# Cross attention: the second shifts between the products with values and those with ones, the second exponential ahead of the queries' eviction

## The chip, the cores and the metric

The kernel runs on one core of one Trainium2 chip. The metric is the device time in microseconds (us); lower is better. Engines are named as in the profile: PE is TensorE (PEld its weight loads), DVE is VectorE, ACT is ScalarE, POOL is GpSimd, SP is SyncE.

## The reference

A decoder of two layers on x of 32 batches x 128 rows x 128 channels. Layer 0 has self attention, cross attention to a context of 32 x 128 x 96, and gated experts; layer 1 has causal attention, a cross attention with latents, and routed experts. The change touches only the cross attention of layer 0:

```python
q = (query @ Wq + bq).reshape(B, Nq, H, D).transpose(0, 2, 1, 3)         # query: layernorm(x)
k = (key_value @ Wk + bk).reshape(B, Nkv, H, D).transpose(0, 2, 1, 3)    # key_value: ctx_768
v = (key_value @ Wv + bv).reshape(B, Nkv, H, D).transpose(0, 2, 1, 3)
attn = jnp.einsum('bhqd,bhkd->bhqk', q, k) * scale
attn = jnp.clip(attn, -CLAMP, CLAMP)
attn = jax.nn.softmax(attn, axis=-1)
x = jnp.einsum('bhqk,bhkd->bqhd', attn, v).reshape(B, Nq, Cq)
return x @ Wo + bo          # 16 heads of 8 channels; added to x
```

## The kernel before

One function, `attention`, does self and cross attention in one phase (and causal attention in a later one). The work goes by batch: numbers 0 to 31 are the batches of self attention, 32 to 63 those of cross attention. Four batches make a group, for which queries, keys and values are projected together.

Each engine runs its own list of steps, in order, and the lists are written out by hand in `ORDERS` (line 220 for cross attention). A step has a lead: in `AHEAD` (line 294), T and f0 at place n of the list work on batch n, s0 on batch n+2, w on batch n-1, y and a on batch n-2. A step written as `q^3` works on a whole group, three batches ahead of the group's first. So "round n" of all engines is T(n) and what stands around it. Semaphores between the engines do the rest: an engine that waits lets nothing behind the waiting step pass.

The steps that matter, with their lines:

- T, `key_scores` (TensorE, L437 to L442): twelve products, scores of batch n with keys on the partitions, into four banks of PSUM (`T` in the code). There is one set of these banks, so T(n) waits until both exponentials of batch n-1 have read them. It ends with four matmuls of L442.
- x0 and x1, `clip_scores` (VectorE, L636): clip to the bounds, in place, two banks each.
- s0, s1, `scores` (TensorE, L422): scores with queries on the partitions, two banks each time, for the maxima two batches ahead. m0, m1, `head_max` (VectorE, L630) reduce them; s1 waits for m0, as both use the same banks.
- mc (GpSimd, L811) clips the maxima; m on TensorE (L467) transposes them into the bank `OM`, and m on ScalarE (L564) copies them out, negated, as shifts.
- f0, f1, `shift` (TensorE, L454): two matmuls each that add the negated maxima of a query to all its scores, in two banks. f0 waits for x0, f1 for x1.
- e0, e1, `exps` (ScalarE, L557): the exponentials of two banks. e0 waits for f0, e1 for f1.
- w, `weigh` (TensorE, L488): 16 products of the exponentials of batch n-1 with the values, then 16 with ones (the sums of the softmax), both into halves of `OM`, and one semaphore at the end. w is free to start when e1 of n-1 is done and the maxima are copied out of `OM`.
- n, `normalise` (VectorE): waits for w; the reciprocal of the sums (L656) and the product with the heads (L660).
- y (TensorE, L501): the output projection of batch n-2; a (VectorE, L722) adds it to x.
- k, q, v on TensorE (L391 to L393): projections of a group, into one bank `PB` that y, the transposes and all projections share: each waits until the user before has been read out. k and q on ScalarE (L576) read keys and queries out of it, v on VectorE (L679) the values; kh and qh (L585) round them.
- mo (VectorE, L693 and L697): the moments of a later group's rows. km on GpSimd (L788) masks the keys by head.

The lists of a round were, with the leads applied: TensorE T s0 (k) m y (x) f0 w (q) f1 s1 (c) (v); ScalarE m (xh) (kh) e0 (q qh) e1 (ch) (ln) (k); VectorE (cs cl) x0 (mo) a x1 m0 (xl) n m1 (qs) (ks) (v). Steps in brackets come in one round of four; those of q, qh and mo in rounds 33, 37, 41 and so on (mo until 53, q until 57).

Of the kernel before, what the change touches and what calls it, by code (L numbers as in the profile page):

```python
# [18 lines left out]
ACT, ALU, AX = mybir.ActivationFunctionType, mybir.AluOpType, mybir.AxisListType  # L19

P = 128
B, D, DC = 32, 128, 96
H, DH = 16, 8
GB = 4
# [4 lines left out]
U = 4  # L29
# [84 lines left out]
def load_setup(nc, x, weights, cols, rows, consts, later, sb, sem, ready, routed):  # L114

    with ExitStack() as ctx:
# [102 lines left out]
    },  # L219
    "cross": {  # L220
# [4 lines left out]
    },  # L225
    "causal": {
# [14 lines left out]
def attention(nc, phase, kinds, sb, bank, context=None, x_ready=None):  # L241
# [27 lines left out]
    V, V_SUMS, maxes, head_ones = sb["v"], sb["v_sums"], sb["maxes"], sb["head_ones"]  # L269

    def one_pass(n):
        return kind(n) in ONE_PASS
# [9 lines left out]
    S, T = bank[:, 0:2 * GT], bank[:, 2 * GT:6 * GT]  # L282
    OM, PB = bank[:, 6 * GT:7 * GT], bank[:, 7 * GT:8 * GT]
# [5 lines left out]
    def t_bank(u):  # L289
# [1 line left out]

    AHEAD = {"T": 0, "f0": 0, "f1": 0, "y": -2, "s0": 2, "s1": 2, "m": 1, "w": -1, "e0": 0, "e1": 0, "x0": 0, "x1": 0,
             "m0": 2, "m1": 2, "n": -1, "a": -2, "mc": 1, "q0": 1, "q1": 1, "km2": 2, "km": 3}

    def steps(engine):


        for n in range(-10, NBT + 2):  # L300
            found = []
            for number, k in enumerate(kinds):
                order = ORDERS[k][engine].split()
                for place, step in enumerate(order):
                    name, _, lead = step.partition("^")
                    first = n + int(lead) if lead else n + AHEAD[name]
                    if first // B == number and not (lead and first % GB):
                        found.append((place / len(order), number, name, first // GB if lead else first))
            for _, _, name, i in sorted(found):
                yield name, i  # L310
# [15 lines left out]
    with ExitStack() as ctx:  # L326
        def buf(name, shape, dt=F32):
            return ctx.enter_context(nc.sbuf_tensor(f"{kinds[0]}_{name}", shape, dt))
# [20 lines left out]
        probs = [buf(f"probs{j}", [P, U, U, P]) for j in range(2)]  # L349
# [28 lines left out]
        def rows_of(u):  # L378
            return slice(32 * u, 32 * u + 32)
# [9 lines left out]
        def _(pe):  # L389
# [5 lines left out]
            def heads_free(n):  # L395

                if n > 0:
                    pe.wait_ge(heads_read if one_pass(n - 1) else heads_done, n)
# [13 lines left out]
            def scores(n, pair):  # L412
                causal = kind(n) == "causal"
                if pair == 0:
                    pe.wait_ge(k_masked, n + 1)
                if 2 * n + pair > 0:
                    pe.wait_ge(max_done, 2 * n + pair)
                units = (2 * pair, 2 * pair + 1)
                if causal:
                    hide([S[:, u * GT:(u + 1) * GT] for u in range(2)], P)  # L420
                for u in units:
                    mm = pe.matmul(s_bank(u), kq_hi[QUERY][(n // GB) % 2][rows_of(u), batch_cols(n)],  # L422
                                   k_hi_m[n % 2][rows_of(u), :, :], start=not causal, stop=True)
                mm.then_inc(scored, 1)

            def key_scores(n):
                causal, clip = kind(n) == "causal", kind(n) == "cross"
                pe.wait_ge(q_masked, 2 * n + 2)
                if n > 0:
                    pe.wait_ge(exp_done, 2 * n)  # L430
                g = (n // GB) % 2
                k_hi, k_lo, q_hi, q_lo = kq_hi[KEY][g], kq_lo[KEY][g], q_hi_m[n % 2], q_lo_m[n % 2]
                if causal:
                    hide([t_bank(u) for u in range(U)], 3 * P)
                out = [t_bank(u).rearrange("p (j q) -> p j q", j=U) for u in range(U)]
                for u in range(U):
                    pe.matmul(out[u], k_hi[rows_of(u), batch_cols(n)], q_hi[rows_of(u), :, :],  # L437
                              start=not causal, stop=False)
                for u in range(U):
                    pe.matmul(out[u], k_hi[rows_of(u), batch_cols(n)], q_lo[rows_of(u), :, :], start=False, stop=False)  # L440
                for u in range(U):
                    mm = pe.matmul(out[u], k_lo[rows_of(u), batch_cols(n)], q_hi[rows_of(u), :, :],  # L442
                                   start=False, stop=clip)
                    if clip and u % 2 == 1:
                        mm.then_inc(keyed, 1)

            def shift(n, pair):
                clip = kind(n) == "cross"
                if pair == 0:
                    pe.wait_ge(neg_max_done, n + 1)  # L450
                if clip:
                    pe.wait_ge(clipped, 2 * (n - B0) + pair + 1)
                for u in (2 * pair, 2 * pair + 1):
                    mm = pe.matmul(t_bank(u), cr[rows_of(u), C_ONES + u * P:C_ONES + (u + 1) * P],  # L454
                                   neg_max[n % 2][rows_of(u), :], start=False, stop=True, skip_group_check=clip)
                mm.then_inc(shifted, 1)

            def transpose_max(n):
                if kind(n) == "cross":
                    pe.wait_ge(max_clipped, n - B0 + 1)  # L460
                else:
                    pe.wait_ge(max_done, 2 * n + 2)
                if n > 0:
                    pe.wait_ge(neg_max_done, n)
                heads_free(n - 2)
                for j in range(U):
                    mm = pe.transpose(OM[:, j * P:(j + 1) * P], maxes[n % 2][:, j * P:(j + 1) * P], sb["ident"][:, :])  # L467
                mm.then_inc(max_transposed, 1)

            def weigh(n):  # L470
                pe.wait_ge(exp_done, 2 * n + 2)
                heads_free(n)
                pe.wait_ge(neg_max_done, min(n + 3, NBT))
                pe.wait_ge(pb_read, pb_uses["v", n // GB])
                if one_pass(n):
                    out = HEADS.rearrange("p (t a c) -> p t a c", a=2, c=32)
                    for j in range(U):
                        for u in range(U):
                            mm = pe.matmul(out[rows_of(u), :, j // 2, :], V_SUMS[(n // GB) % 2][:, n % GB, U * u + j, :],
                                           probs[n % 2][:, u, j, :].rearrange("p (t c) -> p t c", c=32),  # L480
                                           start=j % 2 == 0, stop=j % 2 == 1)
                    mm.then_inc(weighted, 1)
                    return
                for of, c in ((lambda u, j: V[(n // GB) % 2][:, n % GB, U * u + j, :], 0),
                              (lambda u, j: head_ones[:, j, :], P)):
                    for j in range(U):
                        for u in range(U):
                            mm = pe.matmul(OM[rows_of(u), c:c + P], of(u, j), probs[n % 2][:, u, j, :],  # L488
                                           start=j == 0, stop=j == U - 1)
                mm.then_inc(weighted, 1)  # L490

            def bank_free(name, i):
# [4 lines left out]
            def out_project(n):  # L497
                pe.wait_ge(heads_done, n + 1)
                bank_free("y", n)
                c = ATT[kind(n)] * P  # L500
                pe.matmul(PB[:, 0:P], o_t[n % 2][:, :], sb["w_out"][:, c:c + P], start=True, stop=True)\  # L501
                    .then_inc(out_projected, 1)
# [28 lines left out]
            for step, i in steps("PE"):  # L531
                if step == "T":
                    key_scores(i)
                elif step in ("f0", "f1"):
                    shift(i, int(step[1]))
                elif step == "y":
                    out_project(i)
                elif step in ("s0", "s1"):
                    scores(i, int(step[1]))
                elif step == "m":  # L540
                    transpose_max(i)
                elif step == "w":
                    weigh(i)
                elif step == "x":
                    transpose_x(i)
                elif step == "c":
                    transpose_c(i)
                else:
                    project(step, i)
# [2093 lines left out]
```

## Time and profile before

| | us |
|---|---|
| median of three runs | 1313.14 (1307.62 to 1318.99) |
| the profiled execution | 1306.53 |
| its span, first to last instruction | 1304.4 |
| mean granted clock of TensorE | 0.917 |

Shares of the span that each engine was busy: PE 83%, PEld 62%, DVE 73%, ACT 52%, POOL 61%. They are means over six stages with different limits; cross attention takes about a fifth of the span.

A row of a timeline gives the start and the length in us, the engine, the line, the operation, what it writes and reads, the number of instructions merged into the row, and in brackets how long the engine was idle before it and what ended that. An instruction may start a little before the end of the one before it on its engine, so the distance from start to start is the slot that it takes. Ends of matmuls are modelled.

### The profile page before, as it was taken

What the parts mean: (1) busy time and instruction counts of PE and PEld (TensorE: products, weight loads), DVE (VectorE), ACT (ScalarE), POOL (GpSimd) and SP (SyncE); (2) the same over time, 40 slices, a digit from 0 to 9 for tenths busy, and PEclk for the clock granted to TensorE, in tenths of its full rate; (3) what the DMA queues carried; (4) which work ended last, traced back from release to release, by engine and by line L of the source; (5) the groups of instructions that cost most, each with busy time, mean ns of one, the idle gap of its engine ahead of it and who ended that gap; (6) DMA issues with size and microseconds to landing.
All of it is one profiled execution on the core that took longest, in us unless ns stands there. A gap on an engine that the chain in (4) does not pass through costs nothing. (4 is left out here: it accounts for less than half of the span.)

```text
span 1304.4 us, 31319 instructions
## 1 busy us (share of the span) xinstructions
PE 1079.9 (83%) x11009; PEld 807.4 (62%) x11009; DVE 949.6 (73%) x2308; ACT 674.6 (52%) x1306; POOL 797.1 (61%) x895
## 2 busy tenths in 40 slices
PE   1799998888888887699978999994699888299992
PEld 0466665555555555566644666663598887299992
DVE  3598887479999996666644777775599976566764
ACT  2345554334455543345534655654789755166661
POOL 4788885535655651444436767762878687675662
PEclk9999999569999998699996999997799999599996
DMA  9930000000000000000000000000001001367765
GB/s 345 381 130 2 2 2 7 9 15 16 16 16 16 16 10 2 1 1 1 1 1 1 2 3 3 2 3 14 19 8 30 5 26 38 117 197 233 224 213 199
DMA packets 51705, 75.79 MB, mean 58 GB/s; under 512 B 13134, under 2 KB 31699, under 8 KB 51296
## 3 DMA queue, kind: packets, MB, share of 16 engines
q1 hardware_dynamic: 43488, 61.09, 14.7%
q0 software_dynamic: 4544, 8.47, 1.8%
q10 hardware_dynamic: 3520, 4.23, 0.9%
q8 instruction: 90, 1.47, 0.4%
q14 instruction: 63, 0.52, 0.1%
HBM read 40.89 MB, written 31.70 MB: 56 GB/s over the span
## 5 line engine op out<-in xcount | busy, mean ns | idle before, releaser
L630 DVE TENSOR_REDUCE maxes<-bank 128x8 f32<-128x1024 f32 x192 | 233.6, 1217 | 46.8 <-PE bank L422 45.5
L557 ACT ACTIVATE self_probs<-bank 128x1024 f32<-128x1024 f32 x128 | 129.1, 1022 | 45.7 <-PE bank L454 45.3
L788 POOL TENSOR_TENSOR self_k_hi_m<-self_kq_hi,const 128x512 fp32r<-128x512 f32 x64 | 66.5, 1038 | 73.4 <-ACT self_kq_hi L585 73.4
L1540 POOL DMA_INDIRECT returned<-relu_y,relu_slots x78 | 81.0, 1039 | 47.3 <-DVE relu_y L1512 32.8
L564 ACT ACTIVATE self_neg_max<-bank 128x512 fp32r<-128x512 f32 x64 | 38.2, 597 | 135.6 <-PE bank L467 135.6
L1458 ACT ACTIVATE relu_hidden<-bank,cols 128x256 f32<-128x256 f32 x156 | 74.1, 475 | 44.1 <-PE bank L1427 41.0
L1435 PE MATMUL bank<-relu_w_tiles,relu_hidden 128*128 128x128 f32 x624 | 95.0, 275 | 0.0
L1435 PEld LDWEIGHTS bank<-relu_w_tiles,relu_hidden 128*128 128x128 f32 x624 | 83.4, 192 | 0.0
L636 DVE TENSOR_SCALAR bank<-bank 128x1024 f32<-128x1024 f32 x64 | 78.2, 1224 | 3.3 <-PE bank L442 3.2
L2422 POOL DMA_INDIRECT routed<-latent_rows,latent_place_i x64 | 62.6, 978 | 24.4 <-issue 22.2
L454 PE MATMUL bank<-self_neg_max,const_r 32*128 32x512 f32 x256 | 63.7, 488 | 8.8 <-DVE bank L636 5.7
L1314 POOL TENSOR_TENSOR ffn_hidden<-ffn_product,ffn_gate 128x512 f32<-128x512 f32 x32 | 40.9, 1278 | 43.4 <-ACT ffn_gate L1072 35.5
L788 POOL TENSOR_TENSOR self_q_hi_m<-self_kq_hi,const 128x512 fp32r<-128x512 f32 x64 | 66.5, 1040 | 0.2 <-PE bank L454 0.2
L788 POOL TENSOR_TENSOR self_q_lo_m<-self_kq_lo,const 128x512 fp32r<-128x512 f32 x64 | 66.5, 1039 | 0.2 <-issue 0.2
L467 PE MATMUL bank<-ident,maxes 128*128 128x128 f32 x384 | 66.1, 297 | 0.5 <-POOL maxes L811 0.3
L557 ACT ACTIVATE causal_probs<-bank 128x1024 f32<-128x1024 f32 x64 | 63.7, 1022 | 3.6 <-PE bank L454 2.2
L467 PEld LDWEIGHTS bank<-ident,maxes 128*128 128x128 f32 x384 | 43.5, 147 | 33.1 <-issue 26.7
L422 PE MATMUL bank<-self_k_hi_m,self_kq_hi 32*128 32x512 f32 x256 | 60.3, 460 | 4.0 <-DVE maxes L630 2.6
L437 PE MATMUL bank<-self_q_hi_m,self_kq_hi 32*128 32x512 f32 x256 | 33.9, 506 | 34.5 <-ACT self_probs L557 32.8
L788 POOL TENSOR_TENSOR causal_q_lo_m<-causal_kq_lo,const 128x512 fp32r<-128x512 f32 x32 | 33.5, 1047 | 44.8 <-PE bank L454 44.7
L1425 PE MATMUL bank<-relu_s_hi,relu_w_hi 128*128 128x256 f32 x156 | 57.2, 367 | 1.0 <-DVE relu_s_lo L1488 0.9
L2399 POOL TENSOR_TENSOR latent_inverse<-latent_norms_kept,latent_power 128x6 f32<-128x6 f32 x32 | 42.6, 1331 | 13.9 <-DVE latent_norms_kept L2073 13.9
(409 smaller groups left out, 3523.4 us busy)
## 6 DMA issues: line engine op xcount, KB each, us to landing
relu_w_tiles<-in_w_ffn SPq DMA_DIRECT2D x39, 512.0 KB, 3.9
routed<-blank SPq DMA_DIRECT2D x1, 19760.0 KB, 61.4
relu_slots<-routed SPq DMA_DIRECT2D x39, 130.0 KB, 3.1
x_all<-in_x SPq DMA_DIRECT2D x8, 256.0 KB, 8.3
x_before<-x_all SPq DMA_DIRECT2D x8, 256.0 KB
relu_w_tiles<-returned SPq DMA_DIRECT2D x4, 512.0 KB, 8.0
latent_mask_rows<-returned ACTq DMA_DIRECT2D x4, 512.0 KB, 8.5
self_ctx_in<-in_ctx SPq DMA_DIRECT2D x8, 192.0 KB, 2.4
```

The source lines that it names most:

```text
L422: mm = pe.matmul(s_bank(u), kq_hi[QUERY][(n // GB) % 2][rows_of(u), batch_cols(n)], k_hi_m[n % 2][rows_of(u), :, :], start=not causal, sto ...
L454: mm = pe.matmul(t_bank(u), cr[rows_of(u), C_ONES + u * P:C_ONES + (u + 1) * P], neg_max[n % 2][rows_of(u), :], start=False, stop=True, sk ...
L467: mm = pe.transpose(OM[:, j * P:(j + 1) * P], maxes[n % 2][:, j * P:(j + 1) * P], sb["ident"][:, :])
L557: act.activation(probs[n % 2][:, 2 * pair:2 * pair + 2, :, :].rearrange("p u j q -> p (u j q)"), T[:, 2 * pair * GT:(2 * pair + 2) * GT], ...
L630: dve.tensor_reduce(out.rearrange("p j u -> p u j"), S.rearrange("p (u j k) -> p u j k", u=2, j=U), AX.X, ALU.max, negate=True).then_inc(m ...
L636: dve.tensor_scalar(t, t, CLAMP / scale, -CLAMP / scale, ALU.min, ALU.max).then_inc(clipped, 1)
L788: pool.tensor_tensor(out[n % 2][:, :, :], src[(n // GB) % 2][:, batch_cols(n)].bitcast(F32).unsqueeze(1).broadcast_to([P, U, P]), slots.un ...
L1425: pe.matmul(out, w_hi[t % 2][:, of], s_hi[t % 2][:, :], start=True, stop=False)
L1435: mm = pe.matmul(YT[t % 2][b][:, 0:P], hidden[i % C1][:, b * P:(b + 1) * P], w_tile[t % NW][:, F1 + c * P:F1 + (c + 1) * P], start=c == 0, ...
L1458: act.activation(hidden[i % C1][:, :], HT[i % 2][:, 0:TT], ACT.Relu, bias=sb["cols"][:, bass.ds(r + (COL_RELU + c), 1)]).then_inc(hidden_d ...
L1540: pool.indirect_dma_start(returned[:, :], bass.IndirectOffsetOnAxis(ap=slots[t % NX][:, b, P:P + 1].bitcast(I32), axis=0), y[t % NY][:, b, ...
L2422: pool.indirect_dma_start(routed[:, :], bass.IndirectOffsetOnAxis(ap=place_i[u % 3][:, k, b:b + 1], axis=0), rows[G % 4][:, k, n % GB, :], ...
```

## The change

On TensorE, w is cut in two steps: wv, the 16 products with values, with the waits of w, and ws, the 16 products with ones, with the semaphore. f1 stands between them. The projection of the queries, q, stands behind ws, and so behind f1, instead of ahead of f1. On ScalarE, e1 stands ahead of q and qh instead of behind them. On VectorE, the moments mo stand behind a and x1 instead of between x0 and a. No instruction is added or taken away, and no wait. Self and causal attention keep their lists; the cut applies to batches 32 to 62 as weighed in rounds 33 to 63.

```diff
--- before.py
+++ after.py
@@ -218,9 +218,9 @@
         "POOL": "qt^3 bo^6 rs^8 kl^2 km2 kt^4 q1 ql^2 q0",
     },
     "cross": {
-        "PE": "T s0 k^3 m y x^4 f0 w q^3 f1 s1 c^4 v^3",
-        "ACT": "m xh^4 kh^3 e0 q^3 qh^3 e1 ch^4 ln^5 k^4",
-        "DVE": "cs^3 cl^3 x0 mo^7 a x1 m0 xl^4 n m1 qs^1 ks^2 v^3",
+        "PE": "T s0 k^3 m y x^4 f0 wv f1 ws q^3 s1 c^4 v^3",
+        "ACT": "m xh^4 kh^3 e0 e1 q^3 qh^3 ch^4 ln^5 k^4",
+        "DVE": "cs^3 cl^3 x0 a x1 mo^7 m0 xl^4 n m1 qs^1 ks^2 v^3",
         "POOL": "kl^1 ql^1 mc q1 q0 km bo^2 rs^5",
     },
     "causal": {
@@ -291,7 +291,7 @@
 
 
 
-    AHEAD = {"T": 0, "f0": 0, "f1": 0, "y": -2, "s0": 2, "s1": 2, "m": 1, "w": -1, "e0": 0, "e1": 0, "x0": 0, "x1": 0,
+    AHEAD = {"T": 0, "f0": 0, "f1": 0, "y": -2, "s0": 2, "s1": 2, "m": 1, "w": -1, "wv": -1, "ws": -1, "e0": 0, "e1": 0, "x0": 0, "x1": 0,
              "m0": 2, "m1": 2, "n": -1, "a": -2, "mc": 1, "q0": 1, "q1": 1, "km2": 2, "km": 3}
 
     def steps(engine):
@@ -481,12 +481,16 @@
                                            start=j % 2 == 0, stop=j % 2 == 1)
                     mm.then_inc(weighted, 1)
                     return
-                for of, c in ((lambda u, j: V[(n // GB) % 2][:, n % GB, U * u + j, :], 0),
-                              (lambda u, j: head_ones[:, j, :], P)):
-                    for j in range(U):
-                        for u in range(U):
-                            mm = pe.matmul(OM[rows_of(u), c:c + P], of(u, j), probs[n % 2][:, u, j, :],
-                                           start=j == 0, stop=j == U - 1)
+                for j in range(U):
+                    for u in range(U):
+                        pe.matmul(OM[rows_of(u), 0:P], V[(n // GB) % 2][:, n % GB, U * u + j, :], probs[n % 2][:, u, j, :],
+                                  start=j == 0, stop=j == U - 1)
+
+            def weigh_ones(n):
+                for j in range(U):
+                    for u in range(U):
+                        mm = pe.matmul(OM[rows_of(u), P:2 * P], head_ones[:, j, :], probs[n % 2][:, u, j, :],
+                                       start=j == 0, stop=j == U - 1)
                 mm.then_inc(weighted, 1)
 
             def bank_free(name, i):
@@ -539,8 +543,10 @@
                     scores(i, int(step[1]))
                 elif step == "m":
                     transpose_max(i)
-                elif step == "w":
+                elif step in ("w", "wv"):
                     weigh(i)
+                elif step == "ws":
+                    weigh_ones(i)
                 elif step == "x":
                     transpose_x(i)
                 elif step == "c":
```

## Rows read from the trace of the kernel before

**Rows 1.** windows of the steady part: start:end, length, then busy us of PE, PEld, DVE, ACT, POOL

```profile
298.00:498.00 200.00, 165.75 (x2513) 115.56 (x2514) 188.10 (x280) 97.94 (x139) 113.89 (x143) 1.00 0.05 15
```

**Rows 2.** waits, steady part: who waited for whom, us in total, times, longest

```profile
DVE values L679 <- PE bank L393: 2.6, 6, 0.4
DVE self_recip L656 <- PE bank L488: 1.8, 6, 0.3
DVE bank L636 <- PE bank L442: 1.5, 6, 0.2
DVE x_all L722 <- PE bank L501: 1.2, 1, 1.2
PE bank L437 <- ACT self_probs L557: 18.1, 27, 1.0
```

**Rows 3.** timeline, VectorE, batch 43: x0, x1, m0, reciprocal, next x0

```profile
354.51 1.22 DVE L636 TENSOR_SCALAR bank<-bank 128x1024 f32<-128x1024 f32 x1
355.84 1.23 DVE L636 TENSOR_SCALAR bank<-bank 128x1024 f32<-128x1024 f32 x1
356.97 1.22 DVE L630 TENSOR_REDUCE maxes<-bank 128x8 f32<-128x1024 f32 x1
358.33 0.96 DVE L656 RECIPROCAL self_recip<-bank 128x128 f32<-128x128 f32 x1
361.26 1.22 DVE L636 TENSOR_SCALAR bank<-bank 128x1024 f32<-128x1024 f32 x1
```

**Rows 4.** timeline, TensorE, batch 43: f0, values, ones, f1, s1, next T

```profile
355.88 0.50 PE L454 MATMUL bank<-self_neg_max,const_r 32*128 32x512 f32 x2 [0.43 <-ACT self_neg_max L564]
356.31 1.08 PE L488 MATMUL bank<-self_probs,values 128*32 128x128 f32 x32
357.21 1.06 PE L488 MATMUL bank<-self_probs,head_ones 128*32 128x128 f32 x32
358.20 0.50 PE L454 MATMUL bank<-self_neg_max,const_r 32*128 32x512 f32 x2
358.53 0.40 PE L422 MATMUL bank<-self_k_hi_m,self_kq_hi 32*128 32x512 f32 x2
359.90 0.50 PE L437 MATMUL bank<-self_q_hi_m,self_kq_hi 32*128 32x512 f32 x4 [0.97 <-ACT self_probs L557]
```

**Rows 5.** timeline, VectorE, batch 45: moments, a, x1, values step, next x0

```profile
370.49 0.86 DVE L693 BATCH_NORM_STATS2 self_stats<-x_all 128x6 f32<-128x128 f32 x4
371.82 0.29 DVE L722 TENSOR_TENSOR x_all<-bank,x_all 128x128 f32<-128x128 f32 x1
372.03 1.22 DVE L636 TENSOR_SCALAR bank<-bank 128x1024 f32<-128x1024 f32 x1
377.35 0.89 DVE L679 TENSOR_TENSOR values<-bank,rows 128x128 f32<-128x128 f32 x4 [0.43 <-PE bank L393]
378.49 1.23 DVE L636 TENSOR_SCALAR bank<-bank 128x1024 f32<-128x1024 f32 x1 [0.25 <-PE bank L442]
```

**Rows 6.** timeline, TensorE, batch 45: q, v, next T

```profile
374.02 0.49 PE L391 MATMUL bank<-self_x_hi,w_hi 128*128 128x512 f32 x1
375.76 0.33 PE L391 MATMUL bank<-w_hi,self_c_hi 96*128 96x128 f32 x1
377.49 0.51 PE L437 MATMUL bank<-self_q_hi_m,self_kq_hi 32*128 32x512 f32 x4 [0.17 <-ACT self_probs L557]
```

**Rows 7.** timeline, VectorE, batch 57: a, without moments ahead of it

```profile
464.05 0.29 DVE L722 TENSOR_TENSOR x_all<-bank,x_all 128x128 f32<-128x128 f32 x1 [1.24 <-PE bank L501]
```

**Rows 8.** windows (columns as rows 1, then granted clock), and timeline of TensorE, batch 33

```profile
270.00:278.00 8.00, 6.28 (x45) 3.99 (x45) 4.49 (x14) 2.83 (x4) 2.08 (x3) 0.50 0.10 25
...
276.53 1.94 PE L488 MATMUL bank<-self_probs,values 128*32 128x128 f32 x32
278.24 1.93 PE L488 MATMUL bank<-self_probs,head_ones 128*32 128x128 f32 x32
```

**Rows 9.** timeline, VectorE, batch 63: x0

```profile
503.61 1.23 DVE L636 TENSOR_SCALAR bank<-bank 128x1024 f32<-128x1024 f32 x1 [1.30 <-PE bank L442]
```

## The prediction

> **What bounds the kernel now.** I read the busy time of each engine in the cross stage first, then the waits of VectorE and TensorE there, then the timeline of one batch on each engine. Batches are numbered as the program does: 0 to 31 are self attention, 32 to 63 cross attention. The change touches only cross attention, which runs from about 262 to 513 us of the span.
>
> In the steady part, 298 to 498 us, VectorE is busy 188.10 of 200 us, TensorE 165.75, ScalarE 97.94, at a granted clock of 1.00, the 2.4 GHz level [rows 1]. What the reader is to see is that 6% of idle time is all VectorE has to give. Its waits there that the profile names add up to 7.1 us, and the first clip of a batch (x0), the one that needs the new scores, waited for TensorE six times for 1.5 us in all [rows 2]. TensorE itself waited 18.1 us, 27 times, for the second exponential before it could start the next batch's scores [rows 2]. So there are two loops, and they are not equally tight. The scores step T needs e1 of the batch before, and that wait is visible on TensorE. But T's product is next read by VectorE's x0, and x0 stands in VectorE's queue behind m1 of the batch before, which is what sets its time. The wait on TensorE is idle time of an engine that doesn't set the pace.
>
> One plain batch (43) shows the order on VectorE: x0 at 354.51, x1 at 355.84, m0 at 356.97, the reciprocal of n at 358.33 [rows 3]. On TensorE: f0 at 355.88, the products with values at 356.31, those with ones at 357.21, f1 at 358.20, s1 at 358.53, and T at 359.90, after 0.97 us of waiting for e1 on ScalarE [rows 4]. Note the reciprocal: back to back, VectorE starts the next instruction 1.13 us after one of these (355.84 to 356.97), so n could have started at 358.10, and it starts at 358.33. It already waits 0.23 us for the products with ones, which end just before it. There is no slack ahead of n for those products to be later.
>
> **The split of the products (every batch from 33 on).** Nothing is added or removed in number: 16 products with values, 2 shifts, 16 products with ones. Only the order changes, and e1 and n change places as to who is served first. For batch 43:
> - The second shifts need x1, which ends at 357.07 (355.84 + 1.23); the same step after x0 came 0.15 us after the clip's end (354.51 + 1.22 = 355.73, f0 at 355.88), so f1 may start at about 357.22 [rows 3, 4].
> - They stand behind the products with values, whose slot before a shift I take as 0.99 us, as the ones' slot before f1 had it (357.21 to 358.20). So f1 starts at 356.31 + 0.99 = 357.30, which is 0.90 us earlier than before [rows 4].
> - The products with ones then start one slot of shifts later. From a shift to these products the slot is 0.43 us (355.88 to 356.31). That makes 357.73 instead of 357.21: 0.52 us later [rows 4].
> - The reciprocal was waiting for them already, so it starts 0.52 us later, and the sum's second part, the second maxima m1, and x0 of the next batch follow on VectorE at their old distances. The cost is 0.52 us on the path that sets the pace.
> - e1 and with it T can start earlier. This gives nothing back, because x0 stands behind m1, not behind T.
>
> The lower bound of that term takes the slots of pieces of equal shape: 0.90 from values to ones, and 0.33 from f1 to s1 [rows 4]. With these, f1 starts at 357.22, when x1's wait allows it, and the ones at 357.55: 0.34 us later. The upper bound gives the shifts their whole recorded 0.50 us and a gap of 0.10 more, 0.62 us. I take 0.52, since the slots from which it is made are for exactly these neighbours.
>
> The Trainium skill bears on this point, TensorEngine Tiling (Array Packing), Tiling Modes, Key Properties: a change of the tiling mode drains the array. Shifts use 32 rows by 128 columns and the products 128 rows by 32, so the new order changes mode twice more per batch. The slots here agree in size with about 0.1 us for each change (0.43 against 0.33, and 0.99 against 0.90); with that rule the term is 0.52, without it 0.34.
>
> **The moments, moved behind the second clip (five batches: 37, 41, ... 53).** In batch 45 they fill VectorE from 370.49 to 371.82, 1.33 us, between x0 and the addition of the output a, and x1 follows at 372.03 [rows 5]. It looks as if x1 could come 1.33 us earlier. It can't: a stands ahead of x1 and waits for the output projection, which waits for the eviction of the keys. Batch 57 has no moments, and there a waited 1.24 us [rows 7]. So the moments had been covering a stall; moved, the stall is bare and the moments push m0, n and m1 by 1.33 us. Two later waits, 0.43 us ahead of the values step v and 0.25 us ahead of x0, take up 0.68 of that [rows 5]: +0.65 us.
>
> **The queries' projection and eviction (batches 37 to 57, six with the full clock).** The same +0.65 us comes out on TensorE: f1 waits for x1's end (372.03 + 1.22 + 0.15 = 373.40), the ones start 0.43 later, the projection q 0.99 after that, at 374.82 instead of 374.02. The eviction is no longer behind a long queue on ScalarE, but the projection of v needs its bank free, so the 1.74 us from q to v (374.02 to 375.76) remain, and v is 0.80 us later; T saves its 0.17 us wait for e1, which leaves 0.63 [rows 5, 6]. The two paths run side by side, so they are not added: 0.65 us per such batch, batch 57 included by the second path. The mask of the next group's keys on GpSimd comes about as much later with the rounding of the queries; it is used a batch later. Bounds: 0.43 (one slot of shifts), and 1.33 if nothing is taken up.
>
> **The sum.** Batches 34 to 61 are 28: 22 plain x 0.52 = 11.4, and 6 x 0.65 = 3.9, together +15.3 us. Batch 33 runs at the lower clock, where TensorE is the slower engine and the order matters little; the last batches are bound by e1 after all (x0 of batch 63 waited 1.30 us for T [rows 9]), but the products with ones of that batch, and with them n, are late by the slot again. I take both at zero, between -1.3 and +0.5. The bounds are 22 x 0.34 + 6 x 0.43 - 1.3 = +8.8, and 22 x 0.62 + 6 x 1.33 = +22.
>
> The profiled execution took 1306.53 us (span 1304.4, so 2.1 lie around it): with the sum, 1321.8. The three runs shown have a median of 1313.14, that is 6.6 more, and go from 1307.62 to 1318.99. The mean of all four is 1311.6; I put the sum on that: **1327 us**, 1.2% slower.
>
> **Rivals.**
> - Faster: the loop T, clips, f1, e1, T sets the pace. For it: the 18.1 us that TensorE waits for e1 [rows 2]. e1 comes 0.90 us earlier, x 28 = 25 us less, 1287 us. It decides only where VectorE has run dry before x0; it did so in six of 26 batches, for 0.25 us each [rows 2]. Chance 0.06.
> - No measurable change: the slot of shifts costs its lower bound, or n's delay is taken up by waits that I have not seen. +4 to +9 us, about 1318 us. For it: the whole effect is a fraction of a microsecond per batch, and the sum stands close to the limit of 1%. Against it: VectorE has no idle time to take it up. Chance 0.34.
> - The forecast, +10 to +22 us, through VectorE's wait ahead of n. Chance 0.54.
> - Slower still: longer gaps on TensorE bring its clock to the 1.2 GHz level for part of the stage. At a granted clock of 0.50, the values' slot took 1.71 us (276.53 to 278.24) instead of 0.90 [rows 4, 8], so the two groups of products would end 1.6 us later; in a third of 28 batches that is 15 us more, 1342 us. TensorE is busy 83% of the steady part at the higher level [rows 1], and the same work in 7.27 instead of 6.75 us a batch would leave it at 77%. Chance 0.06.
>
> **How the numbers follow.** About 1% is what a measurement of this kernel can tell from no change. Slower by over 1%: 0.54 + 0.06 = 0.60; within 1%: 0.34; faster: 0.06. The range reaches from 1310 (almost the kernel before, so that most of the second rival is in) to 1340 (the upper bound of the sum and the spread of the runs); the forecast's own range is 1321 to 1334.
>
> **What would show it.** In the changed kernel VectorE's wait ahead of the reciprocal should appear in nearly every batch, some 0.7 us by the gap from the end of m0, or 15 us and more over the stage; its wait ahead of a should be about 1.2 us in batches 37, 41, ... 53; TensorE's wait for the second exponential ahead of T should be nearly gone; a plain batch should take 7.2 to 7.3 us from x0 to x0 instead of 6.75 (354.51 to 361.26, [rows 3]). If the reciprocal starts as early as before, the first term falls; if x0 comes earlier in spite of it, VectorE was not the bound; if a no longer waits, the second term falls.

## The result: 4.4% slower, nearly four times the forecast

The changed kernel takes 1371.61 us (four runs, 1370.55 to 1374.83) against 1312.86 us; the ratio is 1.0443, with a 95% interval of 1.0405 to 1.0481. The direction was forecast, the size was not: 1327 us and a range to 1340 us. The profiled execution took 1371.88 us, its span is 1369.8 us against 1304.4, and the mean granted clock of TensorE is 0.880 against 0.917. Here and below a ratio leaves out single runs that were over 1.5% above the fastest of the same kernel, a median does not. Lines behind the cut `weigh` stand six further down (clips L642, maxima L636, reciprocal L662, a L728), and the products are L486 (values) and L492 (ones).

First the part that came as forecast. VectorE in batch 42, a plain one, in the timeline of the changed kernel (columns as in [rows 3]):

```profile
372.32 1.23 DVE L642 TENSOR_SCALAR bank<-bank 128x1024 f32<-128x1024 f32 x1
373.66 1.22 DVE L642 TENSOR_SCALAR bank<-bank 128x1024 f32<-128x1024 f32 x1
374.79 1.22 DVE L636 TENSOR_REDUCE maxes<-bank 128x8 f32<-128x1024 f32 x1
376.72 0.96 DVE L662 RECIPROCAL self_recip<-bank 128x128 f32<-128x128 f32 x1 [0.71 <-PE bank L492]
379.64 1.22 DVE L642 TENSOR_SCALAR bank<-bank 128x1024 f32<-128x1024 f32 x1
```

The reciprocal starts 4.40 us after x0, where it was 3.82 [rows 3], and waits 0.71 us for the products with ones. The next x0 comes 7.32 us after this one instead of 6.75. TensorE in the same batch (to be laid beside [rows 4]):

```profile
373.70 0.50 PE L454 MATMUL bank<-self_neg_max,const_r 32*128 32x512 f32 x2 [0.38 <-DVE bank L642]
374.13 1.08 PE L486 MATMUL bank<-self_probs,values 128*32 128x128 f32 x32
375.14 0.50 PE L454 MATMUL bank<-self_neg_max,const_r 32*128 32x512 f32 x2
375.57 1.08 PE L492 MATMUL bank<-self_probs,head_ones 128*32 128x128 f32 x32
376.58 0.50 PE L422 MATMUL bank<-self_k_hi_m,self_kq_hi 32*128 32x512 f32 x2
376.85 0.51 PE L437 MATMUL bank<-self_q_hi_m,self_kq_hi 32*128 32x512 f32 x4
379.28 0.59 PE L422 MATMUL bank<-self_k_hi_m,self_kq_hi 32*128 32x512 f32 x2 [1.45 <-DVE maxes L636]
```

The slots are 1.01, 0.43 and 1.01 us. T starts 4.53 us after x0 instead of 5.39 and no longer waits for e1. But TensorE did not get faster by that: it now waits 1.45 us ahead of s0, for the maxima that VectorE makes later than before.

Then the part that was not forecast. Rounds of the changed kernel from x0 to x0, as windows (columns as [rows 8]): batches 36, 42, 43, 44, 45 and 49.

```profile
311.63:320.29 8.66, 6.87 (x100) 4.39 (x98) 7.76 (x11) 3.73 (x5) 3.82 (x5) 1.00 0.09 23
372.32:379.64 7.32, 5.49 (x92) 3.67 (x90) 6.57 (x8) 2.65 (x3) 6.50 (x8) 0.99 0.09 36
379.64:389.51 9.87, 8.35 (x92) 5.48 (x90) 6.67 (x9) 4.18 (x7) 4.88 (x9) 0.66 0.01 2
389.51:400.84 11.33, 9.65 (x100) 6.19 (x98) 7.87 (x12) 3.84 (x5) 3.83 (x5) 0.70 0.07 19
400.84:411.79 10.95, 10.04 (x108) 6.90 (x108) 8.26 (x20) 5.06 (x7) 3.03 (x5) 0.84 0.01 2
439.72:449.34 9.62, 8.69 (x108) 6.05 (x108) 8.08 (x21) 5.06 (x7) 3.05 (x5) 1.00 0.01 3
```

The four rounds of the kernel before that answer to batches 42 to 45, in the same view:

```profile
347.76:354.51 6.75, 5.38 (x92) 3.65 (x90) 6.57 (x8) 2.65 (x3) 6.28 (x8) 1.00 0.11 41
354.51:361.26 6.75, 5.32 (x92) 3.65 (x90) 6.57 (x10) 4.15 (x7) 4.87 (x9) 1.00 0.01 2
361.26:369.36 8.10, 6.60 (x100) 4.43 (x98) 7.76 (x12) 3.64 (x6) 3.82 (x5) 1.00 0.11 26
369.36:378.49 9.13, 8.29 (x108) 6.12 (x108) 8.13 (x21) 4.95 (x7) 3.28 (x5) 1.00 0.01 3
```

At a granted clock of 1.00 the rounds are 7.32, 8.66 and 9.62 us against 6.75, 8.10 and 9.13. But in 17 of the 28 rounds from 34 to 61 the clock is below 0.95 (in the kernel before in one, batch 35 at 0.78), and batch 43, with the same list of TensorE as 42, takes 9.87 us. There TensorE's slots are these:

```profile
381.28 0.79 PE L454 MATMUL bank<-self_neg_max,const_r 32*128 32x512 f32 x2
382.00 1.94 PE L486 MATMUL bank<-self_probs,values 128*32 128x128 f32 x32
383.87 0.79 PE L454 MATMUL bank<-self_neg_max,const_r 32*128 32x512 f32 x2
384.59 1.92 PE L492 MATMUL bank<-self_probs,head_ones 128*32 128x128 f32 x32
```

1.87 us from values to f1 and 0.72 from f1 to ones, at the 1.2 GHz level, instead of 1.01 and 0.43. Since the reciprocal has no slack ahead of it, each of these lands on VectorE.

The waits of the changed kernel, 294 to 566 us, name the same chain (columns as [rows 2]):

```profile
DVE self_recip L662 <- PE bank L492: 52.0, 27, 3.3
...
PE bank L422 <- DVE maxes L636: 21.6, 18, 1.5
...
DVE x_all L728 <- PE bank L505: 10.8, 11, 1.6
...
PE bank L467 <- POOL maxes L817: 1.8, 1, 1.8
...
PE bank L437 <- ACT self_probs L563: 0.2, 1, 0.2
```

VectorE's wait for the ones was 1.8 us in all, in the 200 us of [rows 2], and is 52.0 in these 272; TensorE's wait for e1 was 18.1 us and is 0.2.

**Where the 65.4 us of the two spans are.** Batches 34 to 61 took 211.9 us and take 264.1. With every round at its length at the full clock (14 x 7.32, 6 x 8.66, 6 x 9.62, and for 60 and 61 6.71 and 7.12 from the run after_filled_full below) they would take 226.0. So 14.1 us are the longer rounds and 38.1 us the rounds at the lower clock. Ahead of batch 32 the changed kernel is 10.7 us later; 6.1 of that is there before 90 us, where both run the same list, so it is no effect of the change. The other 4.6 come between 219 and 262 us. There the change does reach one round of self attention: in the rounds from one kind to the other the two lists are merged by each step's share of its list's length, and as TensorE's list for cross attention has one step more, the queries' projection of the first group of cross attention stands behind w of batch 28 in round 29 instead of ahead of it. The 4.6 can't be put down to that: in the same stretch the run of the second exponential below, without this exchange, took 3.1 us longer than the kernel before, and the changed kernel with more work on VectorE, which has it, took no longer. Behind batch 63 it loses 2.2 us, and the remaining rounds, 33 and 62, make 0.2.

### The profile page after: what moved, and what is told of

It is laid out like the page before. It is cut to its first block and busy times, and to the rows that moved or that the text cites. A ratio compares the mean times of both kernels' runs of the same rounds, so it can differ in the third digit from the quotient of the medians.

```text
span 1369.8 us, 31319 instructions
## 1 busy us (share of the span) xinstructions
PE 1139.8 (83%) x11009; PEld 839.4 (61%) x11009; DVE 949.1 (69%) x2308; ACT 676.7 (49%) x1306; POOL 798.5 (58%) x895
## 5 line engine op out<-in xcount | busy, mean ns | idle before, releaser
L636 DVE TENSOR_REDUCE maxes<-bank 128x8 f32<-128x1024 f32 x192 | 233.3, 1215 | 51.1 <-PE bank L422 50.4
L422 PE MATMUL bank<-self_k_hi_m,self_kq_hi 32*128 32x512 f32 x256 | 66.5, 511 | 25.4 <-DVE maxes L636 24.1
L454 PE MATMUL bank<-self_neg_max,const_r 32*128 32x512 f32 x256 | 73.5, 566 | 8.5 <-DVE bank L642 5.3
L642 DVE TENSOR_SCALAR bank<-bank 128x1024 f32<-128x1024 f32 x64 | 78.1, 1223 | 0.1
L662 DVE RECIPROCAL self_recip<-bank 128x128 f32<-128x128 f32 x32 | 30.6, 957 | 57.0 <-PE bank L492 57.0
L817 POOL TENSOR_SCALAR maxes<-maxes 128x16 f32<-128x16 f32 x32 | 7.0, 219 | 105.8 <-DVE maxes L636 105.8
L422 PEld LDWEIGHTS bank<-self_k_hi_m,self_kq_hi 32*128 32x128 f32 x256 | 27.7, 205 | 56.7 <-issue 44.8
```

What stands on the lines that cost most here:

```text
L636: dve.tensor_reduce(out.rearrange("p j u -> p u j"), S.rearrange("p (u j k) -> p u j k", u=2, j=U), AX.X, ALU.max, negate=True).then_inc(m ...
L642: dve.tensor_scalar(t, t, CLAMP / scale, -CLAMP / scale, ALU.min, ALU.max).then_inc(clipped, 1)
```

## The experiments

The theory after the result: the cut delays VectorE's reciprocal as forecast (about 15 us), and the rest is TensorE's clock. The rivals: that the waits alone make it, that another part of the change does, or that the clock is a companion and not a cause.

**The cut of the products alone.** Against the changed kernel, q stands ahead of f1 again (and so ahead of the ones too), and ScalarE's and VectorE's lists are those of before:

```diff
-        "PE": "T s0 k^3 m y x^4 f0 wv f1 ws q^3 s1 c^4 v^3",
-        "ACT": "m xh^4 kh^3 e0 e1 q^3 qh^3 ch^4 ln^5 k^4",
-        "DVE": "cs^3 cl^3 x0 a x1 mo^7 m0 xl^4 n m1 qs^1 ks^2 v^3",
+        "PE": "T s0 k^3 m y x^4 f0 wv q^3 f1 ws s1 c^4 v^3",
+        "ACT": "m xh^4 kh^3 e0 q^3 qh^3 e1 ch^4 ln^5 k^4",
+        "DVE": "cs^3 cl^3 x0 mo^7 a x1 m0 xl^4 n m1 qs^1 ks^2 v^3",
```

> The cut of the products alone: f1 between values and ones on TensorE in every round, the queries' projection still ahead of f1, ScalarE's and VectorE's lists as before. Theory (the split moves VectorE's reciprocal by about 0.55 us a batch, and the gaps that this makes on TensorE let its clock fall to 1.2 GHz in the stage): most of the loss, 1345 to 1375 us, mean granted clock of a cross round well under 1.00 in many rounds. Rival A (VectorE's wait alone, and the clock falls because of the moments' or the queries' move): +13 to +16 us, 1326 to 1329 us, clock 1.00 in nearly all cross rounds. Rival B (the split costs nothing by itself): 1313 us.

Measured: ratio 1.0343 (1.0285 to 1.0401), some 45 us, median 1357.82 us, granted clocks of 0.87 to 0.89 where the kernel before had 0.91 to 0.92. Most of the loss comes with the cut alone, as the theory said; rivals A and B fall.

**The moments alone.** The kernel before with VectorE's list of the changed kernel:

```diff
-        "DVE": "cs^3 cl^3 x0 mo^7 a x1 m0 xl^4 n m1 qs^1 ks^2 v^3",
+        "DVE": "cs^3 cl^3 x0 a x1 mo^7 m0 xl^4 n m1 qs^1 ks^2 v^3",
```

> The moments behind the second clip, all else as before. Theory: the addition of the output now waits some 1.2 us in five rounds, and a round with moments takes 0.65 us longer: +3 us, 1316 us, clock as before. Rival (the bare stall in these rounds is what lets the clock fall): +15 us or more and granted clocks under 1.00 in the rounds that follow.

Measured: ratio 1.0066 (1.0025 to 1.0106), 8.7 us, median 1322.70 us. That is between the two expectations. The profile (windows of batches 41 and 45, then VectorE's timeline in batch 37) shows why:

```profile
338.06:347.39 9.33, 8.48 (x108) 6.10 (x108) 7.90 (x20) 4.95 (x7) 2.84 (x5) 1.00 0.01 2
368.98:381.17 12.19, 11.76 (x108) 8.55 (x108) 8.27 (x21) 5.06 (x7) 3.67 (x6) 0.68 0.01 2
```

```profile
309.62 0.29 DVE L722 TENSOR_TENSOR x_all<-bank,x_all 128x128 f32<-128x128 f32 x1 [1.25 <-PE bank L501]
...
315.69 0.87 DVE L679 TENSOR_TENSOR values<-bank,rows 128x128 f32<-128x128 f32 x4
```

The addition a waits 1.25 us, as forecast, but the round is only 0.20 us longer (9.33 against 9.13): the waits behind it, among them that of v, are gone and took up more than I had counted: 1.13 us of the moments' 1.33, where the prediction had 0.68. What makes the time are two rounds, 45 and 57, that lost the clock, some 3 us each, and parts of 46, 47 and 58. Batch 57 has no moments: its list is that of the kernel before.

**The second exponential and the queries alone.** The kernel before with e1 ahead of q and qh on ScalarE, and q behind f1 on TensorE, the products uncut:

```diff
-        "PE": "T s0 k^3 m y x^4 f0 w q^3 f1 s1 c^4 v^3",
-        "ACT": "m xh^4 kh^3 e0 q^3 qh^3 e1 ch^4 ln^5 k^4",
+        "PE": "T s0 k^3 m y x^4 f0 w f1 q^3 s1 c^4 v^3",
+        "ACT": "m xh^4 kh^3 e0 e1 q^3 qh^3 ch^4 ln^5 k^4",
```

> The second exponential ahead of the queries' eviction, and the queries' projection behind f1, with the products uncut. Theory: between -2 and +3 us, since only six or seven rounds have these steps and there the values' projection waits for the eviction; clock as before. Rival (the wait for e1 sets the pace): -5 us or better. Rival (this move is what lets the clock fall): +15 us or more.

Measured: ratio 1.0121 (1.0070 to 1.0172), 15.9 us, median 1328.23 us. I had expected between -2 and +3; the third case came. Batches 37 and 45 as windows:

```profile
316.22:325.58 9.36, 8.42 (x108) 6.10 (x108) 8.14 (x20) 4.95 (x7) 3.05 (x5) 1.00 0.00 1
379.18:391.22 12.04, 11.52 (x108) 8.20 (x108) 8.29 (x20) 5.06 (x7) 3.04 (x5) 0.72 0.01 2
```

The order itself costs 0.23 us a round. Four of these rounds (45, 49, 53, 57) lost the clock for 2.7 to 3.3 us each, and 41, 42 and 50 in part. In batch 45 the clock falls at about 379.6 us, while TensorE is in the keys' projection:

```profile
379.32 0.60 PE L391 MATMUL bank<-self_c_hi,w_hi 96*128 96x512 f32 x1 [0.60 <-DVE self_c_lo L709]
379.71 0.63 PE L392 MATMUL bank<-self_c_lo,w_hi 96*128 96x512 f32 x1
380.14 0.63 PE L393 MATMUL bank<-self_c_hi,w_lo 96*128 96x512 f32 x1
```

The slots are 0.39 and 0.43 us, where the kernel before has 0.33 and 0.24. This is ahead of everything that this kernel moves within the round; the rounds from 42 to 44 have the list of before. So a round can lose the clock with its own instructions unchanged up to that point.

**Idle time filled, 32 rows.** The changed kernel with matmuls that compute nothing, in the wait ahead of s0:

```diff
+            def fill(count):
+                for _ in range(count):
+                    pe.matmul(OM[:, 2 * P:4 * P], cr[0:32, C_ONES:C_ONES + P], cr[0:32, 0:2 * P], start=True, stop=True)
...
                     key_scores(i)
+                    if B0 < i < NBT - 1 and i % GB != 2:
+                        pe.wait_ge(heads_done, i - 1)
+                        fill(4 if i % GB == 1 else 8)
```

> The changed kernel with extra matmuls that compute nothing, between T and s0, where TensorE waits for VectorE's maxima: eight (four in the rounds with the queries' projection) of 32 rows by 128 columns with 256 columns moving, written to a part of a bank that is free. They are behind a wait for VectorE's step n, so they only take idle time. Theory (clock): the granted clock stays near 1.00 through the cross rounds, plain rounds take 7.3 us, those with the queries' projection 9.6, and the time falls to 1325 to 1340 us. Rival (the clock is only a companion, and the loss is in waits): 1365 to 1380 us, since work was added.

Measured: ratio 1.0363 (1.0274 to 1.0451), median 1363.68 us, between the two ranges. One round of four (34, 38, ...) got no such matmuls. The clock was not held. Batches 42 to 45 as windows:

```profile
367.75:375.07 7.32, 6.70 (x100) 4.67 (x98) 6.57 (x8) 2.64 (x3) 6.48 (x8) 1.00 0.09 36
375.07:384.54 9.47, 9.04 (x100) 6.53 (x98) 6.56 (x9) 4.18 (x7) 4.87 (x9) 0.64 0.01 2
384.54:393.21 8.67, 7.32 (x104) 4.99 (x102) 7.77 (x12) 3.73 (x5) 3.82 (x5) 1.00 0.10 25
393.21:405.26 12.05, 11.56 (x108) 7.88 (x108) 8.27 (x21) 5.17 (x7) 3.04 (x5) 0.72 0.01 2
```

TensorE is recorded as busy for 6.70 of 7.32 us in batch 42, and in 43 the clock falls all the same. By itself this run can't tell whether the clock is the cause; the next one has work over the whole array instead.

**Idle time filled, the whole array.** The same, with one change:

```diff
-                    pe.matmul(OM[:, 2 * P:4 * P], cr[0:32, C_ONES:C_ONES + P], cr[0:32, 0:2 * P], start=True, stop=True)
+                    pe.matmul(OM[:, 2 * P:4 * P], cr[:, 0:P], cr[:, 0:2 * P], start=True, stop=True)
```

> The same extra matmuls as in the run after_filled, in the same places, but each over the whole array: 128 rows by 128 columns instead of 32 by 128, 256 columns moving; they compute nothing that is used. With 32 rows TensorE was recorded as busy for 0.91 of a plain round and the clock still fell. Theory (the clock is what costs most, and work over the whole array holds it): granted clock near 1.00 in the cross rounds, plain rounds 7.3 us, 1325 to 1340 us. Rival 1 (no filling of these gaps holds the clock): 1350 to 1370 us, as with 32 rows. Rival 2 (the loss is in waits and not in the clock): clock near 1.00 and still over 1360 us.

Measured: ratio 1.0144 (1.0089 to 1.0199), 18.9 us, median 1332.83 us. Batches 42, 47, 48 and 49 as windows:

```profile
360.35:367.67 7.32, 6.69 (x100) 4.68 (x98) 6.57 (x8) 2.65 (x3) 6.49 (x8) 1.00 0.11 38
403.45:410.77 7.32, 6.64 (x100) 4.68 (x98) 6.57 (x10) 4.30 (x7) 4.88 (x9) 1.00 0.02 3
410.77:419.43 8.66, 7.52 (x104) 4.92 (x102) 7.76 (x12) 3.73 (x5) 3.81 (x5) 1.00 0.10 25
419.43:429.06 9.63, 8.70 (x108) 6.05 (x108) 8.08 (x21) 5.06 (x7) 3.04 (x5) 1.00 0.00 0
```

With the same recorded busy time as with 32 rows (6.69 and 6.70 of 7.32 us in batch 42) the clock holds in all rounds from 35 to 61 but one (45, 12.49 us). Work was added to the changed kernel, nothing else was changed, and it became 39 us faster, as the theory said. That settles it between clock and waits: about 40 us of the 59 are the clock. The other 19 are the order of the work and what this kernel still loses: in its profile rounds 32 and 33 are 3.9 us longer than in the kernel before, and 34 and 45 lost 4.3 us to the clock.

**More work on VectorE in the changed kernel.** One more reduction of 0.6 us in two of four rounds:

```diff
             def sum_lo(G, i):
...
+                dve.tensor_reduce(sb["zeros"][:, c:c + 1], kq_lo[i][G % 2][:, :].bitcast(F32), AX.X, ALU.add)
```

> The changed kernel with one more reduction of 0.6 us on VectorE, whose result is not used, in two of four rounds (behind the sums of the remainders): 1.2 us more of work on the busiest engine in each group of four rounds, 8 us over the stage. Theory A (rounds of one and the same order keep or lose the clock by where in time they fall, so that other distances between rounds can lose less): under 1365 us, with fewer rounds at the lower clock, although work was added. Rival (every added microsecond on VectorE adds up): 1376 to 1382 us.

Measured: ratio 1.0596 (1.0530 to 1.0661), median 1391.22 us. Both expectations were missed: 8 us of work cost about 20, and still more rounds were below a clock of 0.95 (20 of 28, against 17; the mean granted clock is 0.862). That other distances between rounds can lose less was not shown.

**More work on VectorE in the kernel before.** The same line, in one of four rounds (`if i == KEY`):

> The kernel before with one more such reduction of 0.6 us in one of four rounds. VectorE alone gives +4 us, 1318 us, with a granted clock of 1.00 in the rounds from 36 on. Theory A (the kernel before holds its clock only at its own distances between rounds): some of these rounds fall to the lower clock, and the time rises by 10 us or more, 1323 to 1345 us. Rival (it is the order of TensorE's work, or its waits for e1, that held the clock): 1316 to 1320 us.

Measured: ratio 1.0071 (1.0031 to 1.0111), 9.3 us, median 1321.42 us; VectorE's share is 4. Batches 39 and 40 as windows:

```profile
325.86:332.60 6.74, 4.74 (x88) 3.13 (x86) 6.57 (x10) 4.14 (x7) 4.18 (x8) 1.00 0.01 2
332.60:343.38 10.78, 9.44 (x100) 6.43 (x98) 7.86 (x11) 3.76 (x6) 3.94 (x5) 0.68 0.08 21
```

Batch 40 has no instruction more than in the kernel before, where it took 8.10 us at a clock of 1.00. TensorE's list was not touched at all; VectorE was late by 0.6 us in one round of four, and that was enough to lose the clock in batches 40, 45 and 57. Single rounds fell, as theory A has it; the time alone does not decide, as its interval reaches from 4 to 15 us.

**Fillers in the kernel before.** If work over the whole array holds the clock, it may help the kernel before too, in the rounds from self to cross attention, where it runs at 1.2 GHz. Nine such matmuls ahead of T in rounds 26 to 36, into a bank of scores that e0 has read:

```diff
+            def fill(out, count):
+                for _ in range(count):
+                    pe.matmul(out, cr[:, 0:P], cr[:, 0:2 * P], start=True, stop=True)
...
+                    if B0 - 7 < i < B0 + 5 and "cross" in kinds:
+                        pe.wait_ge(exp_done, 2 * i - 1)
+                        fill(t_bank(0)[:, 0:2 * P], 9)
                     key_scores(i)
```

> The kernel before with nine matmuls over the whole array, 256 columns moving, that compute nothing that is used, ahead of T in rounds 26 to 36, where TensorE waits for the second exponential. In the kernel before the clock is at 1.2 GHz from 227 to 282 us, with one short break. Theory (work over the whole array in the waits holds the clock): part of these rounds run at 2.4 GHz and the time falls, 1290 to 1305 us. Rival (the fall comes from the long wait for the context's remainders ahead of the keys' projection, at 228 us, which is not filled): 1310 us and more, since the fillers take twice as long at the lower clock.

Measured: ratio 0.9953 (0.9920 to 0.9986), median 1305.48 us, 6 us faster, by an interval that just leaves out no change; the theory's range ended at 1305, the rival's began at 1310. The window from 227 to 282 us, before and in this kernel:

```profile
227.00:282.00 55.00, 46.15 (x348) 29.96 (x342) 30.68 (x63) 18.32 (x27) 20.05 (x24) 0.53 0.03 9
```

```profile
227.00:282.00 55.00, 43.24 (x439) 31.14 (x437) 33.34 (x69) 21.39 (x31) 20.14 (x24) 0.85 0.05 13
```

The clock rises from 0.53 to 0.85, and the gain is small. In this window TensorE still waits for VectorE, ScalarE and GpSimd; that these waits are the reason is likely, but no run shows it.

The second variant adds sixteen such matmuls ahead of the keys' projection of the first two groups of cross attention, into the bank of the heads, behind the waits that the next step has anyway:

> As before_kept, and sixteen more such matmuls ahead of the keys' projection of the first two groups of cross attention, in the wait for the context's remainders. Theory: the clock stays at 2.4 GHz through most of the change from self to cross attention, 1285 to 1302 us. Rival (other waits in these rounds, on VectorE and GpSimd, are as long): no gain against before_kept, 1305 us or more.

Measured: ratio 0.9974 (0.9941 to 1.0007), median 1307.83 us: no gain beyond the first variant.

## Why the prediction was wrong

- **What bounds the kernel** was right. VectorE sets the pace at the full clock; T came 0.86 us earlier and gave nothing back, and TensorE's idle time moved from T to s0.
- **The cut** was right in mechanism and size while the clock is full: 0.52 us forecast, 0.56 to 0.57 measured in plain rounds. From the values to s1 TensorE takes 2.45 us (slots of 1.01 for the values, 0.43 for f1, 1.01 for the ones) instead of 2.22 (0.90, 0.33 and 0.99 for the same work, [rows 4]): with two changes of shape more, about 0.1 us for each, as the prediction had taken it.
- **The moments and the queries** were mis-sized alone and near together by luck: 0.65 us was put to the round that has both, and with the cut it is 0.49 longer (9.62 against 9.13). The bare stall ahead of a is there, 1.25 us, but alone the moments cost 0.20 and the queries' move 0.23. The slack behind the moments, taken as 0.43 + 0.25 = 0.68, was 1.13 in the run of the moments alone.
- **The sum** of +15.3 us is confirmed by the rounds at the full clock (14.1, and 15.1 against a round before that had itself lost 1 us to the clock), and does not disagree with the run in which the clock was held (+18.9, interval 11.7 to 26.1 from its ratio, some rounds at the lower clock among it).
- **The step that failed is the fourth rival**, "longer gaps on TensorE bring its clock to the 1.2 GHz level". The stage was right, but it got a chance of 0.06, a third of the rounds at 1.6 us each (15 us), and no share in the sum or the range, on the argument that TensorE would still be busy for 77% of a round. The runs showed 17 of 28 rounds below a clock of 0.95, at 1.3 to 2.7 us each, 2.2 on average, 38 us in all. The recorded busy share was no guide. In the changed kernel all seven rounds at 0.75 were at 0.99 or 1.00 themselves (34, 38, ... 58), and each was followed by one that lost the clock; with 32-row fillers rounds at 0.91 were followed by such rounds too, and with 128-row fillers at 0.91 they were not. That the longer gap makes the clock fall, as the rival has it (1.45 us ahead of s0, where 0.97 ahead of T was the longest in the plain round before), is not shown, since the 32-row fillers stood in that gap. And the kernel before was nearer to losing it than its row of 1.00 [rows 1] told: 0.6 us more on VectorE in one of four rounds, or the moments alone, made single rounds fall.
- The range ended at 1340 because that rival was left out of it. With the prediction's own price of 1.6 us in all 28 rounds, 45 us, it would have reached to about 1372.

The Trainium skill tells of a like case in another kernel, in TensorE: Matmul & The Clock Gate, A second HAM failure mode: psum-queue depth-cycling: small idle times between groups of matmuls come so often that the clock gate swings between its two levels. The trace agrees as far as the swing goes: the clock fell 18 times between 291 and 566 us (in the kernel before once between 282 and 497 us), and no wait of the matmuls in the view above is longer than 1.8 us. That the small idle times make it is not shown.

What stays open is what exactly TensorE has to do to keep the clock: rounds with one and the same list kept or lost it in one kernel (49 and 45 of the changed one), fillers of 32 rows did not hold it and fillers of 128 rows did, and no run here tells which property of the fillers it was. Run alone, the three parts cost 45, 9 and 16 us, which sums to 70, where the whole change costs 59; with single rounds that fall or don't, such parts needn't add up.

## What to carry to other kernels

Before an order of steps is changed in a stage that runs at the full clock, price it twice: once at the full clock, by the engine that sets the pace, and once with a share of the rounds at the lower clock, even if the busy share of TensorE looks safe. Afterwards compare rounds of one kind by their granted clock; those at 1.00 give the cost of the order, and the rest is the clock's. An engine's wait that is taken away while another engine sets the pace comes back elsewhere on it, as here from T to s0.

## What was not expected of the hardware

- Matmuls over 128 rows in idle time held the clock and made the kernel some 29 us faster than the same matmuls over 32 rows (ratios of 1.0144 and 1.0363 to the kernel before), at equal recorded busy time (6.69 and 6.70 of 7.32 us in batch 42).
- A delay of 0.6 us on another engine, in one round of four, cost TensorE its clock in later rounds whose instructions were those of before (8.10 to 10.78 us).
